# Key-maximum products cut to 32 rows of the array, with one unit in PSUM at a time

## The reference

```python
query = x @ Wq; keyt = enc @ Wk; valt = enc @ Wv
hs = mha(query, keyt, valt)                      # 2048 queries, 124 keys
ca_q1 = einsum('btc,th->bch', ca, Wq_ca)         # 384 different queries
ca_q1 = ca_q1[:, indices, :]                     # gathered out to 2048
ca_hs1 = mha(ca_q1, x, x)                        # 384 different queries, 2048 keys
ca_q2 = ca_hs1 @ Wq
ca_hs2 = mha(ca_q2, ca @ Wk_ca, ca @ Wv_ca)      # 4 keys
out = (hs + ca_hs2) @ Wout + b_out + x
```

## Time and profile before

| | |
|---|---|
| runs | 853.17, 852.26, 854.06 us; median 853.17 |
| profiled execution | 852.53 us, span 850.8 us |
| TensorE (PE) busy | 793.9 us, 93% of the span |
| weight loads (PEld) busy | 710.5 us, 84% |
| VectorE busy | 525.7 us, 62% |
| ScalarE busy | 382.9 us, 45% |
| GpSimd busy | 166.9 us, 20% |
| products of the units (L959) | 384, 78.2 us busy, 286 ns each |
| reductions of the units (L696) | 192, 131.8 us busy, 688 ns each |

### The profile page before, as it was taken

The page is one execution under the profiler, slowest core; times in us unless marked ns, Lnnn a source line. Parts: engine busy times, 40 slices in busy tenths (PEclk is TensorE's granted clock), DMA queues, the critical chain, the costliest instruction groups (busy, mean ns, idle before and its releaser), DMA issues.

```text
span 850.8 us, 13214 instructions
## 1 busy us (share of the span) xinstructions
PE 793.9 (93%) x5009; PEld 710.5 (84%) x5009; DVE 525.7 (62%) x979; ACT 382.9 (45%) x1036; POOL 166.9 (20%) x231
## 2 busy tenths in 40 slices
PE   6998999999798978999997999999889896999998
PEld 4878999999555658999996999999855555999998
DVE  2345776777799982444433677667789996343442
ACT  1534444444588841333222444444479892122221
POOL 7024722111100001152220311221100000212221
PEclk9999999999799977999999999999979995999999
DMA  8012222322300001444522222223220001244432
GB/s 312 1 27 108 81 81 83 112 89 81 114 1 1 1 29 63 167 143 149 175 75 77 73 90 81 81 93 109 81 75 2 0 1 66 96 152 157 154 112 93
DMA packets 27254, 74.15 MB, mean 87 GB/s; under 512 B 2732, under 2 KB 4268, under 8 KB 27192
## 3 DMA queue, kind: packets, MB, share of 16 engines
q1 hardware_dynamic: 27192, 73.31, 25.2%
HBM read 46.02 MB, written 27.26 MB: 86 GB/s over the span
## 4 chain that ended last, share of the span: by engine, by line
PE 78%; DVE 10%; ACT 5%; issue 5%; DMA 1%; SPq 0%; POOL 0%; POOLq 0%; DVEq 0%
PE PS L984 28%; PE PS L1137 17%; PE PS L1123 9%; PE PS L959 5%; DVE e_lo L784 4%; PE PS L1113 4%; ACT e_hi L569 3%; PE PS L1081 3%; DVE e_hi L778 2%; PE PS L924 2%; PE PS L937 2%; PE PS L902 2%; PE PS L1058 1%; DMA wk_in<-in_L_xattn_Wk_ca 1%; PE PS L1103 1%
## 5 line engine op out<-in xcount | busy, mean ns | idle before, releaser
L984 PE MATMUL PS<-mm_hi,xT_hi 128*128 128x280 f32 (+3 forms) x480 | 162.9, 339 | 1.7 <-DVE xT_lo L655 1.7
L696 DVE TENSOR_REDUCE mpart<-PS 128x4 f32<-128x512 f32 x192 | 131.8, 688 | 49.5 <-PE PS L959 49.5
L984 PE MATMUL PS<-mm_lo,xT_hi 128*128 128x280 f32 (+3 forms) x480 | 157.9, 329 | 0.0
L984 PE MATMUL PS<-mm_hi,xT_lo 128*128 128x280 f32 (+3 forms) x480 | 157.4, 328 | 0.0
L784 DVE TENSOR_TENSOR e_lo<-e,e_hi 128x768 fp32r<-128x768 f32 x128 | 122.9, 979 | 10.0 <-ACT e_hi L569 7.5
L565 ACT ACTIVATE e<-PS 128x768 f32<-128x768 f32 x128 | 104.5, 816 | 20.7 <-PE PS L1058 17.5
L435 POOL TENSOR_TENSOR ex<-ex,rinv 128x992 f32<-128x992 f32 x32 | 59.1, 1847 | 253.7 <-DVE rinv L690 253.5
L984 PEld LDWEIGHTS PS<-mm_hi,xT_hi 128*128 128x128 f32 x480 | 91.2, 190 | 2.6 <-issue 2.5
L984 PEld LDWEIGHTS PS<-mm_hi,xT_lo 128*128 128x128 f32 x480 | 91.4, 191 | 0.3
L984 PEld LDWEIGHTS PS<-mm_lo,xT_hi 128*128 128x128 f32 x480 | 90.8, 189 | 0.2
L521 ACT ACTIVATE ex<-PS,neg 128x124 f32<-128x124 f32 x256 | 89.9, 365 | 2.1 <-DVE neg L663 2.1
(11 more groups left out here) (127 smaller groups left out, 1349.9 us busy)
## 6 DMA issues: line engine op xcount, KB each, us to landing
xin<-in_x SPq DMA_DIRECT2D x64, 320.0 KB, 3.4
ex_kept<-ex SPq DMA_DIRECT2D x32, 512.0 KB, 2.9
ex<-ex_kept SPq DMA_DIRECT2D x32, 512.0 KB, 3.6
out<-res SPq DMA_DIRECT2D x32, 320.0 KB, 2.3
wq_in<-in_L_xattn_Wq SPq DMA_DIRECT2D x2, 800.0 KB, 10.0
wo_in<-in_L_xattn_Wout SPq DMA_DIRECT2D x1, 1600.0 KB, 7.4
wk_in<-in_L_xattn_Wk SPq DMA_DIRECT2D x1, 960.0 KB, 5.5
wk_in<-in_L_xattn_Wk_ca SPq DMA_DIRECT2D x1, 960.0 KB, 7.5
```

The source lines that it names most:

```text
L696: nc.vector.tensor_reduce(mpart[:, n // 2, :, 2 * (n % 2):2 * (n % 2) + 2, i].rearrange("p s k -> p k s"), PS[:, 6 + N % 2, :].rearrange(" ...
L984: last = mul(PS[:, slot(T, k), p0:p0 + w], l[:, i % 2, j, :], rr[:, m0:m0 + w], start=(j == 0 and n == 0), stop=(n == 2), skip_group_check ...
```

## The change

Each of a unit's two products contracts over 32 rows, those of its own head, and no longer over 128. The first product lands in bank 6 and the second in bank 7, 256 columns each. A unit now fills a part of both banks, and TensorE waits ahead of unit N until all N units before it have been reduced. VectorE's reduction takes its 512 numbers out of the two banks. `aTm` is still filled and zeroed as before, and the order of all instructions stays.

```diff
@@ VectorE, unit @@
                     nc.vector.tensor_reduce(mpart[:, n // 2, :, 2 * (n % 2):2 * (n % 2) + 2, i].rearrange("p s k -> p k s"),
-                                            PS[:, 6 + N % 2, :].rearrange("p (k s n) -> p k s n", k=2, s=SETS), AX.X, ALU.max)\
+                                            PS[:, 6:8, 0:G2].rearrange("p k (s n) -> p k s n", s=SETS), AX.X, ALU.max)\
                         .then_inc(mx_made, 1)
@@ TensorE, unit @@
-                    if N >= 2:
-                        pe.wait_ge(mx_made, N - 1)
+                    if N >= 1:
+                        pe.wait_ge(mx_made, N)
                     c, r0 = n // 2, 2 * (n % 2)
                     for k in range(2):
-                        last = mul(PS[:, 6 + N % 2, k * G2:(k + 1) * G2].rearrange("p (s n) -> p s n", s=SETS), aTm[:, r0 + k, c * P:(c + 1) * P],
-                                   gT[:, :, i * P:(i + 1) * P], start=True, stop=True)
+                        rows = slice((r0 + k) * SLOTS, (r0 + k + 1) * SLOTS)
+                        last = mul(PS[:, 6 + k, 0:G2].rearrange("p (s n) -> p s n", s=SETS), aTm[rows, r0 + k, c * P:(c + 1) * P],
+                                   gT[rows, :, i * P:(i + 1) * P], start=True, stop=True)
                     last.then_inc(mx_ps, 1)
```

## The result

The changed kernel takes **911.54 us** (median of 4 runs, 909.97 to 913.51) against 852.71 for the kernel before: a ratio of 1.0688, 95% interval 1.0663 to 1.0714. The profiled execution took 909.97 us, its span is 908.2, so 57.4 more than the 850.8 of before. The forecast was 910, with a range of 865 to 952.

The account below looks back on a forecast made before the run. TensorE, busy for 93% of the span, was taken to bound the kernel. 852.53 us, plus 52 over 30 steps (1.73 each), plus 5 at the stage ends, gave 910 us, range 865 to 952.

Parts of the forecast that it names:

- The hand-off: TensorE waiting for VectorE's reduction between units: about 1.26 us start to start, binding at three closely spaced units per step.
- rival 2: Score-stage units: products don't overlap and shape changes cost nothing; step 10.54 us, 886 us in all; chance 0.16.
- the step on which "most hangs": Score-stage wait: TensorE may no longer start the next unit at 110.17, before the previous unit's reduction ends at 110.34.
- What is removed: Score-stage units on TensorE: two row tiles running at once save 0.12 us per unit without a wait.
- What is added: Row-shape changes between 32-row unit products and 128-row neighbours: two per unit, 384 in all, 0.15 us each.
- w: Cost on TensorE of one row-shape change around a unit: taken as 0.15 us, between 0.10 and 0.28.
- Ends of the stage: Uncovered hand-offs at start and end of the score stage: 2.8 us more per batch, some 5 us in all.
- the clock: TensorE's granted clock: pauses of 0.2 to 0.5 us in the steps should cost none of it; put at nothing.
- Rival 1: Score-stage units: row tiles run at once and shape changes cost nothing; step 10.14 us, 874 us; chance 0.20.
- Rival 3: Score-stage hand-off shortened by short, hidden 32-row loads; at 1.00 us the kernel takes 848 us; chance 0.09.
- A sign that came out against the forecast: PE rows of line 959 in the steps: idle time released by reductions, three per step, starts 1.2 to 1.3 apart.
- the cost of the two far units: Units of a step where nothing waits: some 0.5 us between neighbouring products, instead of 0.24, shows the shape-change cost.

Follow-up runs that it names:

- e1: Kernel before with only the wait for one unit in PSUM and the two banks changed, products still over 128 rows: 891.1 us, ratio 1.044.
- e8: Changed kernel with its units spread to the step products 5, 13, 21, 31, 37 and 43: 911.1 us, ratio 1.067 to the kernel before.
- e3: Changed kernel with both products of a unit on the same 32 rows, so no overlap; second head's maxima left out: 936.0 us, ratio 1.096 to the kernel before.
- e2: Kernel before with both products of a unit on the same 32 rows, no new wait, one bank, second head's maxima left out: 925.1 us, ratio 1.084.
- e11: Kernel before with both products of a unit over the 64 rows of their two heads, everything computed: 928.0 us, ratio 1.084.
- e10: Kernel before, 128-row products, with units moved behind the step products 12 (two), 21, 35 (two) and 43: 854.4 us, ratio 0.999.
- e4: Changed kernel with a unit's two products parted by one step product, so four shape changes per unit: 1079.4 us, ratio 1.265 to the kernel before.

## Why the prediction was right

**The hand-off.** The prediction's arithmetic for products in line (1.17, then 1.27) was measured in e1 as 1.19 and 1.29, and rival 2's step of 10.54 as 10.60. In the changed kernel the bare hand-off is 1.17, not 1.26: I took the second weight load to follow the first by 0.10, and the two run at once. Its role in the changed kernel I had wrong. I let the release come last at the three close places, at the first of them with 1.30 against 1.23 for TensorE itself; measured is that TensorE itself needs 1.24 and the release comes before that (117.87 + 0.05 against 118.00), and spreading the units gains nothing (e8). So the step on which "most hangs" carries none of the 49 us inside the steps. The wait is 38 us alone (e1), and on top of the changes of shape 11 us (e3 against e2), a part of which may be the clock.

**What is removed.** 0.12 per unit through overlap: measured 0.65 / 6 = 0.11 (steps of e3 and after). The factor of 3.07 for four tiles in the Trainium skill ("TensorE: Matmul & The Clock Gate", Part 3) was not run here; its rule agrees in kind, for two tiles did start at once.

**What is added.** w was taken as 0.15 between the bounds 0.10 and 0.28; it is 0.19 by e2. With the second load at nothing the two errors cancel, and that is luck: 0.15 + 0.10 + 0.12 + 0.15 = 0.52 was forecast for a unit, 0.19 + 0.12 + 0.19 = 0.50 is the sum of the measured parts, and 0.51 stands in the trace. With w at 0.19 and all else as I had it, a unit would have been 0.60, the step 0.36 x 6 = 2.16 longer, and the forecast 852.5 + 65 + 5 = 922. The step came out as 11.26 against 11.34. The Trainium skill's rule that a change of tiling mode drains TensorE ("TensorEngine Tiling (Array Packing)", Key Properties) agrees with e2 and e11, which also give its price. That the array really runs empty is the reading that fits, for the next weight load starts 0.09 late and together with its product (the rows of PEld above), and was not shown by itself.

**Ends of the stage.** Forecast 5 us. At the end, from the start of the reduction ahead of the last three to the end of the last one, the kernel before takes 612.85 to 615.88, 3.03; the changed one takes 243.32 to 247.53 in the first stage, 4.21, so 1.18 more, and 4.60 in the second, 1.57 more. At the start, the timeline of PE in the changed kernel:

```profile
69.89 0.46 PE L960 MATMUL PS<-gT,aTm 32*128 32x256 f32 x2 [2.09 <-ACT aTm L542]
71.14 0.58 PE L960 MATMUL PS<-gT,aTm 32*128 32x256 f32 x2 [0.79 <-DVE mpart L696]
72.51 0.58 PE L960 MATMUL PS<-gT,aTm 32*128 32x256 f32 x2 [0.79 <-DVE mpart L696]
73.02 0.60 PE L985 MATMUL PS<-mm_hi,xT_hi 128*128 128x280 f32 x1
```

3.13 us from the first unit to the step, against 1.88, 1.25 more; in the second stage 2.86 against 1.89, 0.97 more. The four together are the 5 us. The other 3 of the 57.4 us I had put at nothing, under "the clock". The windows of the changed kernel show a longer stretch at 1.2 GHz there:

```profile
71.00:85.00 14.00, 13.07 (x64) 10.50 (x65) 7.37 (x17) 4.36 (x20) 3.97 (x9) 0.79 0.10 36
```

and those of the kernel before have the full clock from 74 us on:

```profile
74.00:88.53 14.53, 14.53 (x98) 14.37 (x98) 10.42 (x25) 6.64 (x31) 6.70 (x18) 0.99 0.17 59
```

The stretch at half the clock lasts 6.8 us at the start of both score stages (from 70.1 and from 496.7), in the kernel before 3.4 (from 70.8 and from 466.8). It is a loss of up to 1.7 us per batch. Found outside hand-offs and units is nearly that: from the `g` transposes of step 0 to those of step 1, where the stretch lies, the changed kernel takes 2.9 and 3.4 us more, of which the later start (1.25 and 0.97) and three units (0.8) are 2.1 and 1.8. So 2.4 of the 3 us lie there. Why the clock rises later is not shown.

The total is nearer than its parts, too: 52 + 5 was forecast, 49 + 8 is measured.

**Rivals.** Rival 1 (changes of shape are free) fell with e2: column changes were no guide to row changes. Rival 2's time of 886 belongs to e1, the wait without the row slices, not to the change. Rival 3 needed a hand-off under 1.05; a load of 32 rows is not short (0.18, against 0.19 for one of 128), though two run side by side, and the hand-off is 1.17; but the change of shape comes before it matters. The rows I gave for it don't show short loads either: from 309.9 to 319 us, at half the clock, one load lasts 0.22 on the mean with 49 rows and 0.23 with 128. The 0.09 and 0.20 are their spacings, with products of 49 and of 128 columns behind them.

**A sign that came out against the forecast.** I wrote that the forecast is wrong if no idle time stands ahead of line 959 in the PE rows, and expected three such waits per step. None stands there inside the steps, since the wait on which the sign rests does not bind: the 7.5 us that the page has are the twelve waits at the ends. As a sign of the loss it was badly chosen. The lost time hides in the modelled ends of the records, which overlap it, and shows on PEld and in the spacing of starts only. The other sign, the cost of the two far units, was the good one: 0.51.

No version beat the kernel before; e10 only equals it.

## What to carry to other kernels

Products that use fewer rows than their neighbours pay about 0.38 us for entering and leaving together, so two small products that overlap (0.12 saved) lose by 0.27. Give such a shape its own run of products, long enough that what overlaps is worth more than 0.4 us (an estimate from these prices; no run here reached it), or leave the zeros in and contract over all rows. And costs at one engine don't add up: 38 us for a wait and 72 us for a change of shape made 83 together, so price each alone before you mend the smaller.

## What the runs showed of the hardware that was not expected

- Weight loads of two different row tiles run side by side: two of 32 x 128 in 0.18 us, the length of one.
- A change to 64 rows costs as much as one to 32: 0.39 and 0.38 us per unit with two changes.
- With four changes per unit (e4) the granted clock fell to 0.75 on the mean of 250 us in which PE was recorded busy for 99%.
